# Two heads' maxima in one reduction, GpSimd's first transfers ahead of its memsets, the first weight load in two parts

## What is computed

```
attn = einsum('bqd,bkd->bqk', q * scale, k) + rel_h[..., :, None] + rel_w[..., None, :]
attn = softmax(attn, axis=-1)
out  = einsum('bqk,bkd->bqd', attn, v) ; out @ proj_w + proj_b
```

## Time and profile before

| what | value |
|---|---|
| median of 3 runs | 158.56 us (157.37 to 159.72) |
| the profiled execution | 159.08 us, of which the span of its instructions is 156.4 us |
| TensorE / VectorE / ScalarE / GpSimd busy | 91% / 58% / 45% / 34% of the span |
| granted TensorE clock, mean | 0.998 |
| attention stages of layers 0, 1, 2, 3 begin at | 20.23, 57.21, 102.70, 135.15 us |

### The profile page before, as it was taken

How to read it: one execution, slowest core, us unless ns; L and a number is a source line. 1 busy time by engine, 2 the same in 40 slices (tenths; PEclk the granted TensorE clock), 3 DMA queues, 4 the chain that set the end, 5 groups by cost and what they waited for, 6 DMA issues and landing times.

```text
span 156.4 us, 2663 instructions
## 1 busy us (share of the span) xinstructions
PE 141.6 (91%) x920; PEld 94.2 (60%) x920; DVE 91.1 (58%) x239; ACT 70.7 (45%) x164; POOL 53.1 (34%) x94
## 2 busy tenths in 40 slices
PE   6989589999898958999999999968999999999992
PEld 2569366645457836755458865756666478676550
DVE  2775368736734988876541026666634845697462
ACT  4474127761233216682137713417571445167810
POOL 7689988840200289930000000720000047600000
PEclk9999999999999999999999999999999999999999
DMA  3907648999200156820000000450000017620001
GB/s 84 260 19 184 196 123 262 275 295 298 64 2 0 51 168 96 169 41 0 4 0 0 0 0 2 146 156 4 0 0 0 0 49 212 171 82 0 0 0 50
DMA packets 12508, 13.55 MB, mean 87 GB/s; under 512 B 4144, under 2 KB 10336, under 8 KB 12496
## 3 DMA queue, kind: packets, MB, share of 16 engines
q1 hardware_dynamic: 7792, 9.29, 21.0%
q0 software_dynamic: 3472, 3.01, 8.6%
q10 hardware_dynamic: 1232, 1.08, 2.4%
HBM read 6.82 MB, written 0.20 MB: 45 GB/s over the span
## 4 chain that ended last, share of the span: by engine, by line
PE 62%; DMA 9%; POOL 7%; ACT 7%; DVE 6%; issue 4%; SPq 3%; DVEq 0%; POOLq 0%; ACTq 0%
PE PC L1056 14%; PE RING L1031 9%; PE RING L917 4%; PE RING L995 4%; DMA KS<-KL 4%; PE PA L1066 4%; PE RING L1260 3%; DMA WQKV<-in_w 3%; PE PB L1066 3%; PE PB L995 2%; ACT PR L634 2%; DMA QS<-COLL 2%; SPq L329 2%; PE PA L1266 2%; PE PB L1266 1%
## 5 line engine op out<-in xcount | busy, mean ns | idle before, releaser
L634 ACT ACTIVATE PR<-RING 128x512 f32<-128x512 f32 (+1 forms) x48 | 25.7, 553 | 9.3 <-PE RING L1031 9.1
L917 PE MATMUL RING<-WARM 128*128 128x512 bf16 x84 | 24.7, 406 | 1.3 <-POOL WARM L388 1.3
L1056 PE MATMUL PC<-PR,VX 128*32 128x256 f32 (+1 forms) x192 | 23.6, 369 | 0.1
L827 DVE TENSOR_REDUCE NM<-RING 128x2 fp32r<-128x512 f32 (+1 forms) x32 | 20.1, 652 | 4.1 <-PE RING L995 3.9
L1031 PE MATMUL RING<-QS,KS 128*128 128x256 f32 (+1 forms) x96 | 20.2, 305 | 0.3 <-ACT QS L626 0.2
L1031 PEld LDWEIGHTS RING<-QS,KS 128*128 128x128 f32 x96 | 13.9, 188 | 7.7 <-issue 4.5
L626 ACT ACTIVATE QS<-PA 4x512 fp32r<-4x512 f32 (+1 forms) x20 | 10.6, 531 | 16.5 <-PE PA L1009 16.5
L430 POOL DMA_DIRECT2D QS<-QL x2 | 1.1, 550 | 43.0 <-DVE QL L778 31.0
L827 DVE TENSOR_REDUCE NM<-PB 128x2 fp32r<-128x512 f32 (+1 forms) x16 | 10.5, 654 | 5.6 <-PE PB L995 5.5
L1056 PEld LDWEIGHTS PC<-PR,VX 128*32 128x32 f32 x192 | 8.6, 109 | 8.4 <-ACT PR L634 1.8
L995 PE MATMUL RING<-KS,QS 128*128 128x256 f32 (+1 forms) x64 | 13.2, 298 | 0.0
(11 more groups left out here) (189 smaller groups left out, 271.6 us busy)
## 6 DMA issues: line engine op xcount, KB each, us to landing
WQKV<-in_w SPq DMA_DIRECT2D x2, 576.0 KB, 8.5
WO<-in_wo SPq DMA_DIRECT2D x4, 288.0 KB, 8.8
W<-in_ff SPq DMA_DIRECT2D x2, 576.0 KB, 9.6
KS<-KH ACTq DMA_DIRECT2D x10, 96.0 KB, 3.1
WQKV<-in_w SPq DMA_DIRECT2D x2, 432.0 KB, 5.3
QS<-QHL POOLq DMA_DIRECT2D x12, 64.0 KB, 2.6
KS<-KL SPq DMA_DIRECT2D x8, 96.0 KB, 3.1
QS<-QH SPq DMA_DIRECT2D x8, 96.0 KB, 2.3
```

The lines of the kernel that those rows point to most:

```text
L634: A(PR[:, h % NPR, 0:n], exponents(l, h)[:, 0:n], ACT.Exp).then_inc(sem("probs"), 1)
L827: V.tensor_reduce(NM[:, TURN_OF[h], :, h % GH], MAXIMA[h % 3][:, 0:2 * n_keys].rearrange("p (q k) -> p q k", q=2), AX.X, ALU.max, negate=T ...
L917: M(bank, WARM[:, 0:P], WARM[:, :], start=True, stop=True)
L1056: ins = M(columns(h)[:, reach(l, k)], VX[:, k, h, :], half(PR[:, h % NPR, :], l, k), start=(k == 0 and l != 2), stop=(k == 1), skip_group_ ...
```

## The change

1. SyncE loads the query columns of the layer 0 weights (w0q) as a transfer of its own, ahead of VECS; key and value columns (w0) follow. TensorE waits for w0q before the query matmuls, for w0 before the key matmuls. Five warm-up matmuls instead of seven begin layer 0, and the one between its two statistics matmuls is gone.
2. ScalarE copies the HOT rows of 4 heads instead of 6, VectorE those of 8.
3. GpSimd issues the transfer of ones right after `scale_keys`, then fills VX and NM; ONESC and VR are filled after layer 0's transfers. NM has 12 columns for each half instead of 6 x 32.
4. In layer 1 the first QL transfer goes from GpSimd to SyncE, and so do the twelve transfers of register keys (KRH, KRL), which now stand behind SyncE's moves of layer 1. GpSimd's four mask transfers of 192 KB, behind them before, follow GpSimd's part of the queries directly.
5. VectorE takes the maxima of heads 1 and 2, 4 and 5, 7 and 8, 10 and 11 in one instruction over two neighbouring banks; heads 0, 3, 6 and 9 stay single. `for_maxima` of both heads of a pair waits until the pair before it is reduced. The turns use just the columns of the heads wanted (1 to 4) instead of 32.
6. TensorE's order in the stage is another one; it stands at the end of the diff.

```diff
-HOT_HALF = NH // 2
+HOT_HALF = NH // 3
...
-        NM = sb("NM", [P, len(TURNS), 2, 32], F32R)
+        NM = sb("NM", [P, 2, NH], F32R)
...
+        DOUBLE = ps("DOUBLE", [P, 2 * 512])
+        RINGS = [[DOUBLE[:, i * 512:(i + 1) * 512] for i in range(2)], [ps(f"RING1{i}", [P, 512]) for i in range(2)]]
...
-        MAXIMA = [PB, RINGS[0][1], RINGS[0][0]]
+        MAXIMA = [PB, RINGS[0][0], RINGS[0][1]]
...
+        def turned_rows(t):
+
+            return slice(0, TURNS[t][-1] % GH + 1)
...
-        loads = [("x", X, "xT"), ("gavg", GAVG, "gavg"), ("vecs", VECS, "vecs"), ("w0", WQKV[0], "w0"), ("hot", HOT, "hot"),
+        loads = [("x", X, "xT"), ("gavg", GAVG, "gavg"), ("w0q", WQKV[0][:, :, 0:Q2], "w0q"), ("vecs", VECS, "vecs"), ("w0", WQKV[0][:, :, Q2:Q2 + 2 * C], "w0"), ("hot", HOT, "hot"),
...
-                        if i:
-                            move("ql", rows_of(queries, Q_LOW)[:, heads], QL[:, i, :], "later heads", i + 1)
+                        if i or l == 1:
+                            move("ql", rows_of(queries, Q_LOW)[:, heads], QL[:, i, :], "later heads" if i else "q stack", i + 1)
                         move("kl", rows_of(KS, Q_AGAIN, KEY0, REG1)[:, heads], KL[:, i, :], "later heads" if i else "k stack", i + 1)
+                    if l == 1:
+
+                        sync.wait_ge(sem("kr parts"), 2)
+                        for col in (0, REG1):
+                            for block, src in ((Q_HIGH, KRH), (Q_LOW, KRH), (Q_AGAIN, KRL)):
+                                for i in range(NC):
+                                    sync.dma_start(rows_of(KS, block, col, col + NREG)[:, i * HPC:(i + 1) * HPC].bitcast(F32), src[:, i, :].bitcast(F32))\
+                                        .then_inc(sem("kr stack"), 16)
                     continue
...
-            for n, (tile, value) in enumerate((
-                    (VX[:, :, :, :], 1.0), (NM[:, 0:3].bitcast(F32), 0.0),
-                    (NM[:, 3:6].bitcast(F32), 0.0), (ONESC[:, :], 1.0 / C), (VR[:, :, :], 0.0))):
-                g.memset(tile, value).then_inc(sem("backgrounds"), 1)
-                pool.wait_ge(sem("backgrounds"), n + 1)
-
             pool.wait_ge(sem("hot rows"), 2)
             pool.dma_start(KS[0:GH, :, KEY0:REG1 + NREG], a["ones"]).then_inc(sem("one rows"), 16)
 
+            def background(n, tile, value):
+                g.memset(tile, value).then_inc(sem("backgrounds"), 1)
+                pool.wait_ge(sem("backgrounds"), n)
+
+            background(1, VX[:, :, :, :], 1.0)
+            background(2, NM[:, 0].bitcast(F32), 0.0)
+            background(3, NM[:, 1].bitcast(F32), 0.0)
+
             def move_first_rows(l):
 
-                pool.wait_ge(*upto("ql", l, 1))
-                pool.dma_start(rows_of(QS[l % 2], Q_LOW)[:, 0:HPC].bitcast(F32), QL[:, 0, :].bitcast(F32))\
-                    .then_inc(sem("first rows"), 16)
+                if l == 2:
+                    pool.wait_ge(*upto("ql", l, 1))
+                    pool.dma_start(rows_of(QS[l % 2], Q_LOW)[:, 0:HPC].bitcast(F32), QL[:, 0, :].bitcast(F32))\
+                        .then_inc(sem("first rows"), 16)
...
+                    background(4, ONESC[:, :], 1.0 / C)
+                    background(5, VR[:, :, :], 0.0)
...
-                    pool.wait_ge(sem("kr parts"), 2)
-                    for col in (0, REG1):
-                        for block, src in ((Q_HIGH, KRH), (Q_LOW, KRH), (Q_AGAIN, KRL)):
-                            for i in range(NC):
-                                pool.dma_start(rows_of(KS, block, col, col + NREG)[:, i * HPC:(i + 1) * HPC], src[:, i, :])\
-                                    .then_inc(sem("kr stack"), 16)
...
-                dve.wait_ge(*upto("max psum", l, h + 1))
                 n_keys = WINDOW if l == 2 else T
-                V.tensor_reduce(NM[:, TURN_OF[h], :, h % GH],
-                                MAXIMA[h % 3][:, 0:2 * n_keys].rearrange("p (q k) -> p q k", q=2),
-                                AX.X, ALU.max, negate=True).then_inc(sem("max"), 1)
+                if h % 3 == 0:
+                    dve.wait_ge(*upto("max psum", l, h + 1))
+                    V.tensor_reduce(NM[:, :, h], PB[:, 0:2 * n_keys].rearrange("p (q k) -> p q k", q=2),
+                                    AX.X, ALU.max, negate=True).then_inc(sem("max"), 1)
+                if h % 3 == 1:
+                    dve.wait_ge(*upto("max psum", l, h + 2))
+                    both = DOUBLE[:, :].rearrange("p (h x) -> p h x", h=2)[:, :, 0:2 * n_keys]
+                    V.tensor_reduce(NM[:, :, h:h + 2].rearrange("p q h -> p h q"),
+                                    both.rearrange("p h (q k) -> p h q k", q=2),
+                                    AX.X, ALU.max, negate=True).then_inc(sem("max"), 2)
...
-                    pe.wait_ge(*upto("max", l, h - 2))
-                elif h == 2:
+                    pe.wait_ge(*upto("max", l, h - 2 if h % 3 == 0 else h // 3 * 3))
+                elif h == 1:
                     pe.wait_ge(*upto("v", l, 2))
...
-                    ins = M(turn_bank(t)[0:32, q * P:(q + 1) * P], NM[:, t, q, :], IDR[:, :], start=True, stop=True)
+                    heads = slice(TURNS[t][0] // GH * GH, TURNS[t][-1] + 1)
+                    ins = M(turn_bank(t)[turned_rows(t), q * P:(q + 1) * P], NM[:, q, heads], IDR[:, :], start=True, stop=True)
...
-                keep_warm(free, (7, 3, 3, 3)[l])
+                keep_warm(free, (5, 3, 3, 3)[l])
...
-                    if i == 0:
+                    if i == 0 and l:
                         keep_warm(free, 1)
...
-                loaded(pe, f"w{l}")
+                loaded(pe, f"w{l}" if l else "w0q")
...
+                    loaded(pe, f"w{l}")
...
                 for_maxima(l, 3)
                 turn_maxima(l, 0)
+                scores(l, 0)
                 for_maxima(l, 4)
+                for_maxima(l, 5)
                 turn_maxima(l, 1)
-                scores(l, 0)
-                for_maxima(l, 5)
-                scores(l, 1)
                 for_maxima(l, 6)
                 turn_maxima(l, 2)
+                scores(l, 1)
                 for_maxima(l, 7)
+                for_maxima(l, 8)
                 if l == 2:
                     reg_scores(l, 0)
                 else:
                     values(l, 0, 0)
                 scores(l, 2)
-                for_maxima(l, 8)
                 turn_maxima(l, 3)
                 scores(l, 3)
                 for_maxima(l, 9)
                 if l == 2:
                     values(l, 0, 0)
                 values(l, 0, 1)
+                scores(l, 4)
                 for_maxima(l, 10)
-                scores(l, 4)
+                for_maxima(l, 11)
                 turn_maxima(l, 4)
-                for_maxima(l, 11)
                 scores(l, 5)
                 values(l, 2, 0)
                 values(l, 2, 1)
```

More of the change, by code:

```diff
@@ L156, in build @@
         IDR = sb("IDR", [P, P], F32R)
-        RINGS = [[ps(f"RING{r}{i}", [P, 512]) for i in range(2)] for r in range(2)]
+        DOUBLE = ps("DOUBLE", [P, 2 * 512])
+        RINGS = [[DOUBLE[:, i * 512:(i + 1) * 512] for i in range(2)], [ps(f"RING1{i}", [P, 512]) for i in range(2)]]
         PA = ps("PA", [P, 512])
@@ L284, in build @@
                     "qh": {0: NG, 1: NC, 2: NC, 3: NG}, "ql": {0: NG, 1: NC, 2: NC, 3: NG},
-                    "q stack": {l: (5 if l in REL_LAYERS else 2) * 16 for l in range(LAYERS)},
+                    "q stack": {0: 5 * 16, 1: 3 * 16, 2: 2 * 16, 3: 5 * 16},
                     "k stack": {l: (3 if l in REL_LAYERS else 2) * 16 for l in range(LAYERS)},
@@ L288, in build @@
         signals |= {"later keys": {l: 2 * 16 for l in range(LAYERS)},
-                    "first rows": {l: (4 if l in REL_LAYERS else 2) * 16 for l in range(LAYERS)}}
+                    "first rows": {0: 4 * 16, 1: 16, 2: 2 * 16, 3: 4 * 16}}
         signals |= {"x": {l: 3 * NC if l == 1 else NC for l in range(LAYERS)}, "sums": {0: 1}}
@@ L625, in maxima @@
                 act.wait_ge(*upto("mt psum", l, t + 1))
-                A(QS[l % 2][0:GH, heads[0]:heads[-1] + 1, :], turn_bank(t)[0:GH, None, 0:T].to_broadcast([GH, len(heads), T]),
-                  ACT.Copy).then_inc(sem("mt"), 1)
+                rows = turned_rows(t)
+                A(QS[l % 2][rows, heads[0]:heads[-1] + 1, :],
+                  turn_bank(t)[rows, None, 0:T].to_broadcast([rows.stop, len(heads), T]), ACT.Copy).then_inc(sem("mt"), 1)
             def probs(l, h):
@@ L1380, in layouts @@
         arrays[f"wo{l}"] = by_quadrant(wo[l])
+    arrays["w0q"], arrays["w0"] = arrays["w0"][:, :, 0:Q2], arrays["w0"][:, :, Q2:]
     return {name: np.ascontiguousarray(v, dtype=f32) for name, v in arrays.items()}
```

## The result

| | before | after |
|---|---|---|
| median | 158.86 us (157.37 to 159.72, 4 runs) | 167.62 us (166.97 to 170.28, 4 runs) |
| ratio after to before | | 1.0548, 95% interval 1.044 to 1.0656 |
| profiled execution, its span | 159.08, 156.4 us | 167.92, 166.1 us |
| TensorE / VectorE / ScalarE / GpSimd busy, us | 141.6 / 91.1 / 70.7 / 53.1 | 146.0 / 90.0 / 70.5 / 46.7 |
| granted TensorE clock, mean | 0.998 | 0.979 |

The changed kernel is 5.5% slower, where 1.3% was forecast; 167.62 lies outside the range of 158.2 to 162.7. The page of after shows what the page of before did not: a hole in TensorE's row, and in the PEclk row right behind it a granted clock that falls to half.

The account below looks back on a forecast made before the run. TensorE bounds the kernel, through each layer's first maxima matmul and the chain from it to the first values. Terms: -1.7 + 1.0 (layer 0) + 0.7 (layer 1) + 1.0 + 1.0 = +2.0 us, median 160.6 us, range 158.2 to 162.7.

Parts of the forecast that it names:

- Layer 1: Layer 1's stage: slightly later KL, scores 1 behind head 6, less work done ahead; 0.7 us lost, bounds 0.2 and 1.4.
- I take 61.5, 0.2 later than before: Layer 1: KL for the later heads lands at 61.5, between 61.0 left alone and 61.8 behind all bytes in flight.
- rival A: Layer 1: masks push KL to 62.5 or later, layer 1 pays 1.7 or more; sum +4.0, 162.6 us; chance 0.12.
- a KL transfer that takes over 4 us: Layer 1: a sign named in advance that would show the prediction wrong.
- if all bytes in flight had to pass first: Layer 1: KL at 61.8, from masks 2.5 us plus queries and keys 1.9 us, both from 57.4 on.
- The pairs, layers 0 and 2: Attention stages: TensorE's new order delays turn 1, scores 1 and first values or register scores; 1.0 us lost per layer.
- Layer 3: Layer 3's stage: pays 1.0 us for the maxima of two heads, as layer 0 does; stage of 16.2 us instead of 15.2.
- The start of layer 0: Before layer 0's stage: earlier Q and GpSimd's shorter queue start the first maxima matmul at 18.5, 1.7 us earlier; bounds 1.3, 2.4.
- B: Stages: slack makes up delayed values, 0.2 us a layer remain; sum -0.9, 157.7 us; chance 0.14.
- D: Start of layer 0: COLL lands at layer 3's pace, start at 17.8, 159.9 us; chance 0.14.
- C: Start of layer 0: GpSimd's order brings nothing, COLL lands no earlier than 19.8, gain 0.4 only, 161.9 us; chance 0.1.
- the main case: Whole kernel: layer 0 starts 1.7 us earlier, the stages lose more, sum +2.0 us, 160.6 us; chance 0.5.

Follow-up runs that it names:

- b_masks_first: Before, with GpSimd's four mask transfers of layer 1 issued ahead of its twelve register key transfers: 161.35 us, ratio 1.0241.
- b_kr_on_sync: Before, with the twelve register key transfers moved from GpSimd to SyncE, so that the masks start at 56.4: 162.64 us, ratio 1.0273.
- a_gap_filled: The changed kernel with 19 warm-up matmuls on TensorE ahead of head 6's wait in layer 1: 166.47 us, ratio 1.0464.
- c_order: c_kr_back with TensorE's order of the changed kernel, maxima still single: 162.5 us, ratio 1.0194.
- b_pairs: Before, with the double reductions, narrower turns and TensorE's order of the changed kernel: 162.88 us, ratio 1.0225.
- a_masks_late: The changed kernel, with GpSimd's masks waiting until the later heads' queries and keys of layer 1 have landed: 163.54 us, ratio 1.0208.
- c_single: a_both with single maxima and TensorE's order of before: 159.11 us, ratio 1.0082.
- a_both: a_masks_late with the three warm-up matmuls of layer 0 put back too: 163.17 us, ratio 1.033.
- c_kr_back: c_single with the register key transfers moved back to GpSimd, ahead of the masks: 158.95 us, ratio 1.0014.

## Why the prediction was wrong

**Layer 1, the term that failed.** "I take 61.5, 0.2 later than before", sum 0.7, bounds 0.2 and 1.4. KL landed at 65.54, and the sum was 6.36. The mechanism was named (rival A, and "a KL transfer that takes over 4 us" as what would show it), its size was not. Two steps of the working fell. The first is the length of the masks: 2.5 us was read from the run of nines in the earlier trace rows, which is the busiest part of it only. In before they last from the first issue at 63.05 to the last landing at 68.75 (issued at 64.65, 4.1 us to landing), 5.7 us. Issued from 57.90 on, beside the queries and keys, they take 5.0 us in the median each, and 7.6 us from first issue to last landing. Transfers from 57 to 66 us in after (queue, packets, MB, share of the 16 engines; then issues with KB each and median us to landing):

```profile
q0 software_dynamic: 849, 0.80, 41.2%
q1 hardware_dynamic: 1422, 0.51, 26.2%
...
QS<-in_mask POOLq DMA_DIRECT2D x4, 192.0 KB, 5.0
...
KS<-KH ACTq DMA_DIRECT2D x2, 96.0 KB, 4.3
...
KS<-KL SPq DMA_DIRECT2D x1, 96.0 KB, 6.3
```

All of them are slower at once. KL lands at 65.54, with the last mask, which was issued 0.23 us behind it and lands at 65.47. That is nearest to the case I called "if all bytes in flight had to pass first". With the 57.90 and the 5.7 us in it, that sum gives 57.9 + 5.7 + 1.9 = 65.5, an estimate. That it fits this closely is luck: for b_masks_first (first mask at 57.14) it gives 64.7, and KL landed at 63.19; for b_kr_on_sync (56.39) 64.0, and KL landed at 62.19. It is an upper bound there. The rule of the Trainium skill that I set beside it ("DMA: Bandwidth & Descriptors", Queues, rings and completion order) put KL nearer 61.0 than 61.8. The trace does not agree with that landing, 65.54; how the engines shared their turns among the queues no row shows.

The second step was absent: I asked what is late behind head 6, and not what TensorE does meanwhile. It did nothing for 3.99 us, the granted clock went to 0.50, and a_gap_filled prices that at 2.2 us. Head 6 later by 3.5, half clock 2.2, pairs 0.6: the 6.36.

**The pairs, layers 0 and 2: right.** Forecast 1.0 each, bounds 0.7 and 1.3; measured 1.08 and 1.09. The chain too: turn 1 at 3.3 (3.22), copy 1 at 3.6 (3.54), scores 1 at 4.1 (4.06), values at 5.3 (5.43), the double reduction 1.21 us (1.22). That the order and not the reduction makes it was the forecast's statement, and c_order shows it for the whole loss of layer 2 and for 0.84 of layer 0's 1.08; the other 0.24 comes with the pairing itself. The narrower turns take the 0.28 us of before; nothing came of them, as stated. In layer 1 their part, 0.6 - 0.3 + 0.2 = 0.5 in the forecast, was 0.63 in b_pairs (+16.39), where head 6 waits for KL as in before. The 0.48 of a_masks_late is less because that wait is gone; against c_single, where it is gone too (+15.30), the pairs cost 0.96 (a_both).

**Layer 3: the mechanism right, the sum short.** Forecast 1.0, measured 1.63. In b_pairs, where the ROWL transfer took 2.6 us, the stage takes +16.15, 0.90 more than before; the other 0.73 goes with the late ROWL transfer, of which the forecast had nothing.

**The start of layer 0: wrong in sign.** Forecast 1.7 us earlier (bounds 1.3 and 2.4), measured 0.37 later in the profile of after, 1.0 earlier at best (c_single). The first step is the order of GpSimd's list, which was to bring COLL forward by 1.3 us. With the old order it goes out at 16.69 to 16.80, with the new one and the wide NM of before at 16.67 to 16.88; with the narrower NM at 16.37 in the old order (b_pairs) and at 16.45 to 16.50 in the new one, all warm-ups in place. So the order brings nothing and the narrower NM some 0.3 us. The moved memsets are saved, but the scaling ends at 9.14 to 9.44 instead of 8.90 to 9.03, and the handover to a transfer is paid twice. What then decides the start is the landing, 2.3 to 3.7 us in these kernels (3.3 in before), which no run explains.

In after itself it went like this. Q was forecast at 6.5: it started at 7.69 and at half rate, and the half rate began with the warm-ups; the three taken away were booked as a gain of 0.2 and never asked what they do for the rate behind them. With the warm-ups back Q started at 6.61 in c_kr_back, nearly as forecast, and COLL still went out at 16.69. The first query transfer was forecast at 10.9: it was 11.97, because GpSimd's scaling ended at 9.23 instead of 8.97, and two handovers from a GpSimd instruction to a transfer took 0.42 and 0.44 us, where I had counted 0.1 and none. COLL was forecast at 15.45: the ROWL and COLH transfers ahead of it had waits of their own (0.37 and 0.24 us), since the late Q made those tiles late, and it went out at 17.16.

**Rivals.** B, where the stages pay little, has nothing for it in any run. D's landing came once, in c_single (2.3 us), but from an issue at 16.67. C (the GpSimd order brings nothing) describes the start better than the main case did, and its reason isn't the one that I gave: GpSimd's list did not get earlier, by the later scaling and the second handover. A names the place of the loss. Its 1.7 us were less than a third of it.

Put together, the 10.16 us of the stages are: the pairs and their order 3.7 (1.08, 0.62, 1.09 and 0.90), the late KL with the half clock 5.7 in layer 1, the late ROWL 0.7 in layer 3. Open are why KL took 6.3 and not 4.9 us, and what makes ROWL late.

## What to carry to other kernels

When a transfer is pulled forward, take its length from first issue to last landing, not from the busiest slices, and add it to every transfer that is then in flight: here that sum was met in after, and it was 1.5 and 1.8 us too long in two other kernels. A queue that is free is not a path that is free. Where a wait on the engine that bounds the kernel grows to several microseconds, price the slower matmuls behind it as well as the wait. And when work is paired, write down where each consumer of the first half stands in the new order: here a cheaper instruction came with 0.9 to 1.1 us more in layers 0, 2 and 3, most of it by what had to be moved in front of its users, and moving one of them back brought 0.1 us in layer 2.

## What was not expected of the hardware

- After an idle stretch of 3.99 us TensorE's granted clock was 0.50 for more than 4 us although TensorE was busy 4.37 of 4.40 us; with 19 warm-up matmuls in that stretch it stayed at 1.00. A wait of 2.21 us was followed by 0.50 in b_kr_on_sync, one of 2.46 us by 1.00 in b_masks_first.
- In the first microseconds the page's clock says 1.00 (0.998 in the mean of before) and yet the matmuls ran at half the rate: the second group of seven warm-ups in 3.15 us in after, 1.88 in before (the first seven of before take 3.17 too). The PEclk row of after has a 9 there. A duration per matmul is the better witness.
- The 96 KB of KL for the later heads took 2.2 to 3.0 us from issue to landing without the masks in flight, 4.6 and 4.9 with them (b_kr_on_sync, b_masks_first), and 5.7 to 6.3 in after and the two kernels built on it that keep the early masks.
- GpSimd's step from its own memset or multiplication to the issue of a transfer behind it took 0.42 to 0.44 us in after (0.31 in before, and 0.30 in c_single, both behind a larger memset).
- The ROWL transfer for heads 4 to 7 of layer 3 landed after 2.6 to 3.2 us in seven kernels and 3.9 to 4.2 us in the other seven. What decides between the two is open.
